# Fourth layer's sums turned by DMA instead of by TensorE in a four-layer graph network

## Chip, cores and metric

The kernel runs on one core of one Trainium2 chip. The metric is the device time of one execution in microseconds (us). Engines are called by the names of the profile: PE is TensorE's matmul, PEld its weight load, DVE is VectorE, ACT is ScalarE, POOL is GpSimd, SP is SyncE.

## What is computed

x is 3327 nodes by 256 features, adj a 3327 by 3327 matrix of zeros and ones. Four graph layers follow one another, each on `h = max(layernorm(x), 0)`, each added to x. The first is a graph attention, the second a normalized graph convolution, the third one with signs of weights and activations. The fourth, which the change touches, is

```
def _L3_gnn_ref(x, adj, t, weight):
    ts = t[0]
    support = x @ weight
    return (1.0 - ts) * support + ts * (adj @ support)
h = jnp.maximum(_layernorm(x, axis=-1), 0.0)
x = x + _L3_gnn_ref(h, adj, L3_gnn_t, L3_gnn_weight)
```

The kernel computes it as `z = (1 - ts) h + ts (adj @ h)`, then `x + z @ weight`.

## The kernel before

The 3327 rows are padded to 26 tiles of 128 nodes (`TILES`). In the fourth layer h is held in `x_layer[3]` as two f16 halves, a high part and the rest, so that the products are as exact as f32 asks for. For each tile t of 128 output rows TensorE makes 26 matmuls (`add3`, line 1495, one for each block j of 128 nodes), whose 512 columns are the 256 of the high half and the 256 of the low one. One f8 matrix block of the adjacency is the weight of each. They add up in one of four PSUM banks (`quarter`). `tile3` (line 1498) is the loop over j.

Then comes what the code calls the epilogue of tile t, on all engines while TensorE is already in tile t + 1:

- DVE `product` (lines 1866, 1869, 1871) makes z in `y_sb`, f32, from the two halves of the bank and the product `tb` that ACT made (line 1191), and raises `z_done[3]`.
- PE `layer_epilogue`, part 0, at j = 13 of the next tile: `turn` (line 1302) transposes z, two f32 matmuls with an identity of 128 by 128 each, into the PSUM bank `ep`, and raises `zt_psum[3]`.
- ACT `turned_copy` (line 1196) makes the high f16 half of the turned z in `zt16`, DVE `low3` (line 1910) the low one, and raises `zt_done[3]`.
- PE `layer_epilogue`, part 1, at j = 20 of the next tile: six f16 matmuls with the weight's halves `w3_16` (line 1376) into the bank `op`, then `p_done[3]`.
- DVE `update` (line 1903), in its order after `product` of the next tile, adds x and writes `xo`; SP stores it (line 823).

Which j a step stands at is written out by hand: `EPILOGUE_AT`, `LATE_AT` for tiles 2 and 3, `STEADY_AT` for all later ones. A value is (how many tiles back, which part, first or not).

DVE's order for tile t is `product(t)`, `update(t - 1)`, `low3(t)`, `check`. `check` (line 1856) goes over a half row block of the f32 adjacency in `gb`; the others of that kind have been done in the layers ahead. ACT's order is `turned_copy(t - 1)`, `product(t)`.

SP issues, when the matmuls of tile t are done (`mm_done[3]`): for odd t up to 17 one pair of adjacency tiles in f8, 832 KB, from a scratch tensor in HBM (`load_slot`, line 863); for each t up to 23 the next half row block for `check`, 832 KB (line 817); and the store of tile t - 2, 128 KB (line 823). All three run on SP's queue, q1 in the profile. ACT's queue (q10) carries five small loads at the very start and nothing else. ACT issues DMAs in its own instruction order.

Of the kernel before, what the change touches and what calls it, by code (L numbers as in the profile page):

```python
# [7 lines left out]
P = 128  # L8
# [458 lines left out]
def fast_program(nc, io, general, prefix="f_"):  # L467


    with ExitStack() as ctx:  # L470
# [3 lines left out]
        def sem(name):  # L474
            return ctx.enter_context(nc.semaphore(prefix + name))
# [40 lines left out]
        y_sb = sb("y_sb", [P, 2, 2 * F])  # L516
# [12 lines left out]
        xo = s_f32[:, 2304:2816].rearrange("p (r f) -> p r f", r=2)  # L529
        sign_w = s_flat[:, 5632:6144].rearrange("p (c f) -> p c f", c=FB)  # L530
        ident16 = s_flat[:, 6144:6272]
        binary = s_flat[:, 11264:11264 + 4 * F].rearrange("p (r f) -> p r f", r=4)
        w1_16 = s_flat[:, 8192:8192 + 4 * F].rearrange("p (h c f) -> p h c f", h=2, c=FB)
        binary_t = s_flat[:, 6784:7040]
# [162 lines left out]
        group_here = [sem(f"group_here{b}") for b in range(2)]  # L697
        yh_done = sem("yh_done")
        extra_here = [sem(f"extra_here{b}") for b in range(2)]
        slot_here = [sem(f"slot_here{b}") for b in range(4)]  # L700
        yl_done = sem("yl_done")
        w1_done = sem("w1_done")
# [66 lines left out]
        with nc.Block() as block:  # L769
# [197 lines left out]
            def _(a):  # L967
# [220 lines left out]
                def product(t, p, s):  # L1188
                    if not (isinstance(t, int) and t < 2):
                        a.wait_ge(z_done[3], t - 1)  # L1190
                    a.activation(tb[:, p * F:(p + 1) * F], x_layer[3][:, bass.ds(t, 1), F:2 * F].rearrange("p a f -> p (a f)"),
                                 ACT.Copy, scale=omt_scaled[:]).then_inc(tl_done[3], 1)

                def turned_copy(t):
                    a.wait_ge(zt_psum[3], t + 1)
                    a.activation(zt16[:, 0], ep[:, 0:F], ACT.Copy, scale=Z3).then_inc(zt_hi, 1)  # L1196

                def pair(k, s, first=False):
                    for p in range(2):
                        t = 2 * k + p  # L1200
                        if not (first and p == 0):
                            turned_copy(t - 1)
                        if first and p == 0:
                            product(0, 0, s)
                            product(1, 1, s)
                        if not first:
                            product(t, p, s)
                pair(0, 1, True)
                with a.Fori(0, PAIRS // 2) as k:
                    for i in range(2):  # L1210
                        pair(2 * k + 1 + i, i)
                turned_copy(TILES - 1)


            @block.tensor
            def _(pe):
# [139 lines left out]
                all_pairs(pe, pair)  # L1356

                def layer_epilogue(layer, t, p, part, first=False):
                    if part == 0:
                        turn(t, p, ep, zt_psum[layer], z_done[layer], FB)  # L1360
                    else:

                        if first:
                            pe.wait_ge(read_o[1], TILES)
                            pe.wait_ge(late_w, 64)
                        else:
                            pe.wait_ge(read_o[layer], t)
                        if layer == 1:
                            project(t, op, w_sb[layer], FB, zt_done[layer], p_done[layer])
                            return  # L1370
                        if first:
                            pe.wait_ge(w3_done, 2)
                        pe.wait_ge(zt_done[3], t + 1)
                        for c in range(FB):
                            for half, w_half in ((0, 0), (0, 1), (1, 0)):
                                mm = pe.matmul(op[:, 0:F], zt16[:, half, c * P:(c + 1) * P], w3_16[:, w_half, c, :],  # L1376
                                               start=(c + half + w_half == 0), stop=(c == FB - 1 and half == 1))
                        mm.then_inc(p_done[3], 1)

# [161 lines left out]
            def _(v):  # L1541
                def settle():

                    v.sem_inc(waited, 1)
# [314 lines left out]
                for layer in L:  # L1859
# [47 lines left out]
                    def low3(t):  # L1907

                        v.wait_ge(zt_hi, t + 1)
                        v.scalar_tensor_tensor(zt16[:, 1], ep[:, 0:F], Z3, zt16[:, 0], ALU.mult, ALU.subtract)\  # L1910
                         .then_inc(zt_done[3], 1)

                    def norm(t, p):

# [5 lines left out]
                    def pair(k, first, last=False, r=0):  # L1920
                        for p in range(2):
# [11 lines left out]
                            if layer == 3 and not (first and p == 1):  # L1933
                                product(t, p, r)
                                if first and p == 0:
                                    product(1, 1, r)
                                    low3(0)
                            if not (first and p == 0):

                                update(t - 1, 1 - p, k if p else k - 1, first)  # L1940
                            if layer == 3 and not (first and p == 0):
                                low3(t)
# [107 lines left out]
```

## Time and profile before

| | |
|---|---|
| median of 3 runs | 964.89 us (964.3 to 965.39) |
| profiled execution, whole | 965.67 us |
| its span, from first to last instruction | 964.0 us |
| PE busy | 933.9 us, 97% of the span |
| DVE busy | 743.3 us, 77% |
| ACT busy | 540.9 us, 56% |
| POOL busy | 94.1 us, 10% |
| mean granted TensorE clock | 0.988 of full |

Busy shares are means over four layers with different limits, so each stage is read from its own stretch of the trace. The fourth layer is the stretch from 779 us to the end; its steady tiles run from about 812 to 945 us.

### The profile page before, as it was taken

Reading aid. Unit: us, or ns where it says so; the run is one execution under the profiler, and the core shown is the slowest. Engines: PE = TensorE matmul, PEld = TensorE weight load, DVE = VectorE, ACT = ScalarE, POOL = GpSimd, SP = SyncE. Lnnn points to the kernel's source line nnn. Section 1 sums busy time; section 2 is a strip of 40 time slices with the busy share of each in tenths; the row PEclk is TensorE's granted clock in tenths of the full one; section 3 lists DMA queues with packets and bytes.
Section 4 is the critical chain, followed back from the end, with each engine's and each line's share of the span. In section 5 each row is a group of like instructions: output and inputs, shape, how many; then the busy total and the mean of one; then the engine's idle time right before and its main releaser. Section 6 shows DMA issues by size and latency. Waiting matters only on the chain.

```text
span 964.0 us, 18964 instructions
## 1 busy us (share of the span) xinstructions
PE 933.9 (97%) x7105; PEld 689.2 (71%) x7105; DVE 743.3 (77%) x1112; ACT 540.9 (56%) x934; POOL 94.1 (10%) x206
## 2 busy tenths in 40 slices
PE   9889999999999999999999999999999989999995
PEld 8457788888888888888888455555788845555553
DVE  7697899999999999999996776656447755655664
ACT  6476899999999999999985611111223331111010
POOL 4100001000010001000030000000024430000000
PEclk9899999999999999999999999999999999999998
DMA  4915276677576666658312425655247726666642
GB/s 178 96 45 77 23 100 76 66 89 96 48 96 83 81 66 86 86 51 109 46 39 100 173 94 203 211 183 203 114 181 281 276 79 213 215 227 205 201 153 65
DMA packets 39883, 120.80 MB, mean 125 GB/s; under 512 B 4604, under 2 KB 24597, under 8 KB 39701
## 3 DMA queue, kind: packets, MB, share of 16 engines
q1 hardware_dynamic: 27653, 97.94, 29.0%
q0 software_dynamic: 10944, 21.30, 25.5%
q10 hardware_dynamic: 1232, 0.85, 0.3%
q8 instruction: 32, 0.52, 0.2%
q14 instruction: 22, 0.18, 0.1%
HBM read 169.48 MB, written 14.50 MB: 191 GB/s over the span
## 4 chain that ended last, share of the span: by engine, by line
PE 84%; DVE 7%; ACT 3%; issue 2%; POOL 2%; DMA 0%; POOLq 0%; DVEq 0%; ACTq 0%
PE f_ya L1318 23%; PE f_yb L1318 23%; PE f_ya L1495 14%; PE f_ya L1433 12%; DVE f_gb L1856 2%; PE f_ya L1269 2%; PE f_yb L1404 2%; PE f_yb L1376 2%; PE f_yb L1269 1%; PE f_ya L1442 1%; POOL f_gv L960 1%; ACT f_ubuf L1184 1%; ACT f_x_mat L1186 1%; DVE f_stats L1600 1%; PE f_yb L1302 1%
## 5 line engine op out<-in xcount | busy, mean ns | idle before, releaser
L1318 PE MATMUL f_ya<-f_x_mat,f_s_mat 128*128 128x257 f16 x2028 | 334.6, 273 | 1.9 <-DVE f_x_mat L1664 1.9
L1318 PE MATMUL f_yb<-f_x_mat,f_s_mat 128*128 128x257 f16 x2028 | 333.2, 273 | 0.0
L1318 PEld LDWEIGHTS f_yb<-f_x_mat,f_s_mat 128*128 128x128 f16 x2028 | 198.2, 98 | 24.8
L1318 PEld LDWEIGHTS f_ya<-f_x_mat,f_s_mat 128*128 128x128 f16 x2028 | 194.5, 98 | 27.2 <-issue 2.8
L1030 ACT ACTIVATE f_gb<-f_e_tile,f_expc 128x256 f32<-128x256 f32 x338 | 144.5, 494 | 9.3 <-DVE f_s_mat L1694 9.3
L1856 DVE SCALAR_TENSOR_TENSOR f_gb<-f_gb 128x1664 f32<-128x1664 f32 x52 | 97.7, 1886 | 18.0 <-DMA f_gb<-adj_dram 18.0
L1689 DVE SCALAR_TENSOR_TENSOR f_s_mat<-f_wm,f_s_mat 128x1792 f16<-128x1792 f32 (+1 forms) x52 | 98.4, 1892 | 12.1 <-ACT f_s_mat L1041 8.5
L1683 DVE TENSOR_TENSOR f_wm<-f_gb,f_a 128x1792 f32<-128x1792 f32 (+1 forms) x52 | 98.1, 1887 | 3.2 <-issue 1.6
L1684 DVE SCALAR_TENSOR_TENSOR f_gb<-f_gb,f_a 128x1792 f32<-128x1792 f32 (+1 forms) x52 | 98.1, 1887 | 0.0
L1694 DVE SCALAR_TENSOR_TENSOR f_s_mat<-f_gb,f_s_mat 128x1792 f16<-128x1792 f32 (+1 forms) x52 | 98.0, 1886 | 0.0
L1041 ACT ACTIVATE f_s_mat<-f_wm 128x1792 f16<-128x1792 f32 (+1 forms) x52 | 82.5, 1587 | 22.0 <-DVE f_wm L1683 20.9
L1196 ACT ACTIVATE f_yt_sb<-f_yb 128x256 f16<-128x256 f32 x26 | 10.0, 384 | 145.2 <-PE f_yb L1302 145.2
L1495 PE MATMUL f_ya<-f_x_mat,f_wm 128*128 128x512 f16 x364 | 85.5, 385 | 3.6 <-DVE f_x_mat L1916 3.2
L1047 ACT ACTIVATE f_s_mat<-f_gb 128x1792 f16<-128x1792 f32 (+1 forms) x52 | 82.5, 1587 | 7.0 <-DVE f_gb L1684 6.9
L1433 PE MATMUL f_ya<-f_wm,f_x_mat 128*128 128x512 fp8e4 (+1 forms) x416 | 84.6, 352 | 0.0
L1056 ACT ACTIVATE f_rows<-f_rows 128x1664 fp8e4<-128x1664 fp8e4 x48 | 75.5, 1574 | 0.0
L1433 PE MATMUL f_ya<-f_a,f_x_mat 128*128 128x512 fp8e4 x312 | 73.1, 379 | 0.0
L1495 PE MATMUL f_ya<-f_x_mat,f_a 128*128 128x512 f16 x312 | 71.7, 379 | 0.0
L1495 PEld LDWEIGHTS f_ya<-f_x_mat,f_wm 128*128 128x128 fp8e4 x364 | 35.9, 99 | 42.6 <-DVE f_x_mat L1916 4.0
L1433 PEld LDWEIGHTS f_ya<-f_wm,f_x_mat 128*128 128x128 f16 x416 | 40.2, 98 | 32.6
L928 POOL DMA_DIRECT2D f_a<-adj_t_dram x52 | 28.4, 546 | 303.7 <-PE f_yb L1318 263.4
L1483 PE MATMUL f_ya<-f_s_mat,f_a 128*128 128x256 f16 x468 | 52.5, 272 | 3.5 <-DMA f_a<-f_a_dram 2.2
(185 smaller groups left out, 938.2 us busy)
## 6 DMA issues: line engine op xcount, KB each, us to landing
f_gb<-adj_dram SPq DMA_DIRECT2D x52, 832.0 KB, 5.0
f_a<-f_a_dram SPq DMA_DIRECT2D x23, 832.0 KB, 5.9
f_wm<-f_a_dram SPq DMA_DIRECT2D x16, 832.0 KB, 4.6
f_rows<-adj_dram POOLq DMA_DIRECT2D x24, 416.0 KB, 8.2
f_a<-adj_t_dram POOLq DMA_DIRECT2D x26, 224.0 KB, 4.9
f_a_dram<-f_a SPq DMA_DIRECT2D x26, 224.0 KB, 5.3
f_a<-adj_t_dram POOLq DMA_DIRECT2D x26, 192.0 KB, 6.9
f_a_dram<-f_a SPq DMA_DIRECT2D x26, 192.0 KB, 4.2
```

The costliest lines, as they stand in the source:

```text
L1030: made = a.activation(blocks(gb, c)[:, j - lo, :], e_tile[:, r, :], ACT.Copy, scale=expc[:, 0, j:j + 1])
L1041: a.activation(weights(c, 2), blocks(wm, c), ACT.Copy, scale=DOWN).then_inc(hm_done, 1)
L1047: a.activation(weights(c, 0), blocks(gb, c), ACT.Copy, scale=UP).then_inc(hp_done, 1)
L1056: a.activation(part_of, part_of, ACT.Copy, saturate=False, accum_out=row_parts[:, r, c:c + 1])\
L1318: return pe.matmul(bank[:, 0:F + 1], s_mat[:, j, side, i], x_mat[:, j, x_side, 0:F + 1], start=start, stop=stop)
L1433: mm = pe.matmul(turned_sum(g, f), x_layer[1][:, j, half * F + f * P:half * F + (f + 1) * P], wide[g % 2][:, 0:width(g) // HP, j, :], star ...
L1495: return pe.matmul(quarter[2 * s + p][:, 0:2 * F], slots3[slot][:, j, p * P:(p + 1) * P], x_layer[3][:, j, 0:2 * F], start=(j == 0), stop= ...
L1683: v.tensor_tensor(part(wm, c), part(gb, c), a8_part(r, c), ALU.min).then_inc(wm_done, 1)
L1684: v.scalar_tensor_tensor(part(gb, c), part(gb, c), 1.0, a8_part(r, c), ALU.max, ALU.mult).then_inc(wp_done, 1)
L1689: v.scalar_tensor_tensor(weights(c, 3), blocks(wm, c), DOWN, weights(c, 2), ALU.mult, ALU.subtract)\
L1694: v.scalar_tensor_tensor(weights(c, 1), blocks(gb, c), UP, weights(c, 0), ALU.mult, ALU.subtract)\
L1856: v.scalar_tensor_tensor(gb[:, half, 0:HW], gb[:, half, 0:HW], 0.0, gb[:, half, 0:HW], ALU.is_gt, ALU.not_equal, accum_out=bad[:, bass.ds( ...
```

## The change

In the fourth layer, for every tile but the last, z is no longer turned by TensorE. ACT makes the high f16 half of z straight from `y_sb` into a new buffer `z16`, DVE's `low3` makes the low half there too, and ACT issues, for each half and each of the two 128-column blocks, one transposing DMA (`transpose=True`) from `z16` to `z16_t`: two when the high half is there, and two after it has waited for DVE's low half. They are of 128 by 128 f16, 32 KB each, all four on one semaphore of the tile's parity, `z16_here[p]`. PE's six matmuls of line 1376 take their weights from `z16_t`, and stand at j = 24 of the next tile instead of j = 20, behind a wait for that semaphore. Nothing stands at j = 13. The first tiles are moved too: tile 0's six matmuls go to j = 22 of tile 2, tile 1's to j = 8 of tile 3, tile 2's to j = 24 of tile 3. ACT now makes `product(t + 1)` after it has issued the four transfers of tile t. Tile 25 goes the old way.

```diff
+                def high_part(t, p, n, reuse=True):
+
+                    a.wait_ge(z_done[3], t + 1)
+                    if reuse:
+                        a.wait_ge(z16_here[p], 64 * n)
+                        a.wait_ge(p_done[3], t - 1)
+                    a.activation(z16[:, p, 0, :], y_sb[:, p, 0:F], ACT.Copy, scale=Z3).then_inc(zt_hi, 1)
+                    a.wait_ge(zt_hi, t + 1)
+                    settle()
+                    for half in range(2):
+                        if half == 1:
+                            a.wait_ge(zt_done[3], t + 1)
+                            settle()
+                        for c in range(FB):
+                            a.dma_start(z16_t[:, p, half, c, :], z16[:, p, half, c * P:(c + 1) * P], transpose=True)\
+                             .then_inc(z16_here[p], 16)
...
-                pair(0, 1, True)
-                with a.Fori(0, PAIRS // 2) as k:
+                product(0, 0, 1)
+                product(1, 1, 1)
+                high_part(0, 0, 0, False)
+                high_part(1, 1, 0, False)
+                with a.Fori(0, PAIRS // 2 - 1) as k:
                     for i in range(2):
-                        pair(2 * k + 1 + i, i)
+                        for p in range(2):
+                            t = 4 * k + 2 + 2 * i + p
+                            product(t, p, i)
+                            high_part(t, p, 2 * k + 1 + i)
...
-                        pe.wait_ge(zt_done[3], t + 1)
+                        if at_end:
+                            pe.wait_ge(zt_done[3], t + 1)
+                        else:
+                            pe.wait_ge(z16_here[p], 32 * (t - p) + 64)
+                            settle()
                         for c in range(FB):
                             for half, w_half in ((0, 0), (0, 1), (1, 0)):
-                                mm = pe.matmul(op[:, 0:F], zt16[:, half, c * P:(c + 1) * P], w3_16[:, w_half, c, :],
+                                turned_z = zt16[:, half, c * P:(c + 1) * P] if at_end else z16_t[:, p, half, c, :]
+                                mm = pe.matmul(op[:, 0:F], turned_z, w3_16[:, w_half, c, :],
...
-                LATE_AT = ({13: (2, 0, False), 20: (2, 1, True)},
-                           {3: (2, 0, False), 8: (2, 1, False), 15: (1, 0, False), 22: (1, 1, False)})
-                STEADY_AT = {EPILOGUE_AT[3][i]: (1, i, False) for i in range(2)}
+                LATE_AT = ({22: (2, 1, True)}, {8: (2, 1, False), 24: (1, 1, False)})
+                STEADY_AT = {24: (1, 1, False)}
...
+                            v.scalar_tensor_tensor(z16[:, p, 1, :], y_sb[:, p, 0:F], Z3, z16[:, p, 0, :], ALU.mult, ALU.subtract)\
+                             .then_inc(zt_done[3], 1)
```

## Rows read from the trace of the kernel before

**Rows 1.** The page: busy time of each engine, and shares of the chain.
```profile
PE 933.9 (97%) x7105; PEld 689.2 (71%) x7105; DVE 743.3 (77%) x1112; ACT 540.9 (56%) x934; POOL 94.1 (10%) x206
PE 84%; DVE 7%; ACT 3%; issue 2%; POOL 2%; DMA 0%; POOLq 0%; DVEq 0%; ACTq 0%
```

**Rows 2.** The chain in order of time, from 720 us: start, us, what.
```profile
825.59 1.51 PE f_ya L1495 x7
827.10 0.66 PE f_yb L1376 x6
827.75 4.10 PE f_ya L1495 x19
832.07 1.51 PE f_ya L1495 x7
```

**Rows 3.** The timeline, 844.8 to 858.2 us: start, us, engine, line, what.
```profile
847.04 4.26 PE L1495 MATMUL f_ya<-f_x_mat,f_wm 128*128 128x512 f16 x19
...
848.53 0.33 SPq L863 DMA_DIRECT2D f_wm<-f_a_dram  x1
848.66 0.48 DVE L1869 SCALAR_TENSOR_TENSOR f_y_sb<-f_ya,f_t_scaled,f_s_mat 128x256 f32<-128x256 f32 x1 [0.52 <-PE f_ya L1495]
...
849.18 0.48 DVE L1871 SCALAR_TENSOR_TENSOR f_y_sb<-f_ya,f_t_scaled,f_y_sb 128x256 f32<-128x256 f32 x1
...
849.58 0.41 DVE L1903 SCALAR_TENSOR_TENSOR f_s_mat<-f_yb,f_xs 128x256 f32<-128x256 f32 x1
...
855.02 0.33 SPq L817 DMA_DIRECT2D f_gb<-adj_dram  x1
```

**Rows 4.** Groups by line, 700 to 964 us: count, busy us, mean ns, idle before.
```profile
L1302 PE MATMUL f_yb<-f_ident,f_y_sb 128*128 128x128 f32 x52 | 10.0, 274 | 1.2 <-DVE f_y_sb L1871 1.2
...
L1184 ACT ACTIVATE f_ubuf<-f_xs,f_down 128x256 f32<-128x256 f32 x26 | 13.2, 508 | 52.4 <-POOL f_cst L963 52.4
...
L1866 DVE SCALAR_TENSOR_TENSOR f_s_mat<-f_x_mat,f_omt_scaled,f_s_mat 128x256 f32<-128x256 f32 (+1 forms) x26 | 12.5, 481 | 0.1
```

**Rows 5.** DMA issues, 780 to 964 us: count, KB each, median us to landing.
```profile
f_wm<-f_a_dram SPq DMA_DIRECT2D x5, 832.0 KB, 4.5
f_a<-f_a_dram SPq DMA_DIRECT2D x4, 832.0 KB, 4.5
out_dram<-f_s_mat SPq DMA_DIRECT2D x25, 128.0 KB, 4.8
out_dram<-f_s_mat SPq DMA_DIRECT2D x1, 112.0 KB, 1.7
```

**Rows 6.** Stretches of 0.5 us; last columns: granted clock, DMA share, GB/s.
```profile
850.80:851.30 0.50, 0.50 (x5) 0.31 (x4) 0.00 (x0) 0.00 (x0) 0.00 (x0) 1.00 1.01 426
...
853.80:854.30 0.50, 0.50 (x4) 0.24 (x3) 0.50 (x3) 0.00 (x0) 0.00 (x0) 1.00 0.97 398
...
855.30:855.80 0.50, 0.50 (x4) 0.25 (x3) 0.47 (x2) 0.00 (x0) 0.00 (x0) 1.00 0.00 0
...
859.30:859.80 0.50, 0.50 (x7) 0.39 (x5) 0.50 (x1) 0.00 (x0) 0.00 (x0) 1.00 0.28 100
```

**Rows 7.** The start: page's queue row, landings (0 to 15 us), ACT's issues.
```profile
q10 hardware_dynamic: 1232, 0.85, 0.3%
...
f_s_mat<-w_att_t_dram ACTq DMA_DIRECT2D x1, 256.0 KB, 5.2
...
f_a_sb<-a_vec_dram ACTq DMA_DIRECT2D x1, 2.0 KB, 7.4
...
0.74 0.47 ACTq L971 DMA_DIRECT2D f_s_mat<-w_att_t_dram  x1
1.23 0.48 ACTq L972 DMA_DIRECT2D f_a_sb<-a_vec_dram  x1
...
2.23 0.81 ACTq L974 DMA_DIRECT2D f_wtrans_sb<-wtrans_dram  x1
```

**Rows 8.** Stretches of 2 us where TensorE waits; columns as in rows 6.
```profile
785.00:787.00 2.00, 0.23 (x1) 0.00 (x0) 0.73 (x3) 0.85 (x2) 1.60 (x6) 1.00 0.00 0
...
789.00:791.00 2.00, 2.00 (x6) 0.73 (x5) 0.77 (x2) 0.65 (x2) 0.00 (x0) 0.50 0.00 0
```

More of the change, by code:

```diff
@@ L531, in fast_program @@
         ident16 = s_flat[:, 6144:6272]
+        z16 = s_flat[:, 9216:9216 + 4 * F].rearrange("p (r h f) -> p r h f", r=2, h=2)
+        z16_t = s_flat[:, 10240:10240 + 4 * F].rearrange("p (r h c i) -> p r h c i", r=2, h=2, c=FB)
         binary = s_flat[:, 11264:11264 + 4 * F].rearrange("p (r f) -> p r f", r=4)
@@ L699, in fast_program @@
         extra_here = [sem(f"extra_here{b}") for b in range(2)]
+        z16_here = [sem(f"z16_here{b}") for b in range(2)]
         slot_here = [sem(f"slot_here{b}") for b in range(4)]
@@ L1194, in turned_copy @@
                 def turned_copy(t):
-                    a.wait_ge(zt_psum[3], t + 1)
+                    a.wait_ge(zt_psum[3], 1)
                     a.activation(zt16[:, 0], ep[:, 0:F], ACT.Copy, scale=Z3).then_inc(zt_hi, 1)
[L1198 to L1207, printed above, removed]
@@ L1212, in _ @@
+                for t in range(TILES - 4, TILES):
+                    product(t, t % 2, t // 2 % 2 ^ 1)
+                    if t < TILES - 1:
+                        high_part(t, t % 2, t // 2)
                 turned_copy(TILES - 1)
@@ L1358, in layer_epilogue @@
                 def layer_epilogue(layer, t, p, part, first=False):
+                    at_end = isinstance(t, int) and t == TILES - 1
                     if part == 0:
-                        turn(t, p, ep, zt_psum[layer], z_done[layer], FB)
+                        if at_end:
+                            turn(t, p, ep, zt_psum[layer], z_done[layer], FB)
                     else:
@@ L1372, in layer_epilogue @@
                             pe.wait_ge(w3_done, 2)
-                        pe.wait_ge(zt_done[3], t + 1)
+                        if at_end:
+                            pe.wait_ge(zt_done[3], t + 1)
+                        else:
+                            pe.wait_ge(z16_here[p], 32 * (t - p) + 64)
+                            settle()
                         for c in range(FB):
                             for half, w_half in ((0, 0), (0, 1), (1, 0)):
-                                mm = pe.matmul(op[:, 0:F], zt16[:, half, c * P:(c + 1) * P], w3_16[:, w_half, c, :],
+                                turned_z = zt16[:, half, c * P:(c + 1) * P] if at_end else z16_t[:, p, half, c, :]
+                                mm = pe.matmul(op[:, 0:F], turned_z, w3_16[:, w_half, c, :],
                                                start=(c + half + w_half == 0), stop=(c == FB - 1 and half == 1))
@@ L1905, in update, with low3 @@
                             v.nop().then_inc(read_o[3], 1)
-                    def low3(t):
+                    def low3(t, p):
                         v.wait_ge(zt_hi, t + 1)
-                        v.scalar_tensor_tensor(zt16[:, 1], ep[:, 0:F], Z3, zt16[:, 0], ALU.mult, ALU.subtract)\
-                         .then_inc(zt_done[3], 1)
+                        if isinstance(t, int) and t == TILES - 1:
+                            v.scalar_tensor_tensor(zt16[:, 1], ep[:, 0:F], Z3, zt16[:, 0], ALU.mult, ALU.subtract)\
+                             .then_inc(zt_done[3], 1)
+                        else:
+                            v.scalar_tensor_tensor(z16[:, p, 1, :], y_sb[:, p, 0:F], Z3, z16[:, p, 0, :], ALU.mult, ALU.subtract)\
+                             .then_inc(zt_done[3], 1)
                     def norm(t, p):
@@ L1936, in pair @@
                                     product(1, 1, r)
-                                    low3(0)
+                                    low3(0, 0)
                             if not (first and p == 0):
@@ L1941, in pair @@
                             if layer == 3 and not (first and p == 0):
-                                low3(t)
+                                low3(t, p)
                             if layer == 3 and not first and not (last and p == 1):
```

## The prediction, made blind

> **What bounds the kernel now.** I read the page first: PE is busy for 97% of the span and the chain that ended last runs over PE for 84% [rows 1]. Means of four layers say little about one, so next the chain in order of time, from 720 us on. In the fourth layer it repeats one pattern: 7 matmuls of line 1495, six of line 1376, 19 of line 1495, and again, with nothing but PE between [rows 2]. The reader is to see the small hole: 827.75 + 4.10 is 831.85, and the next piece starts at 832.07. Those 0.22 us are the two transposes of line 1302, which the chain leaves out as too short. One tile takes 832.07 - 825.59 = 6.48 us, and 26 x 0.216 (4.10 us / 19) + 0.66 + 0.216 is 6.49: there is no idle time in it. The layer goes at the pace of PE's instructions, so what is taken off PE is gained, and what PE waits for is lost in full.
>
> Next the timeline of one tile, for when z is there. In [rows 3] the 19 matmuls that start at 847.04 are the last 6 of one tile and the first 13 of the next, so the next tile begins at 847.04 + 6 x 0.216 = 848.34. I call that T, and count from it. DVE's first product starts at 848.66 and the second ends at 849.66: z is there at T + 1.32. SP issues its load at 848.53, T + 0.19.
>
> **What is removed.** 25 of the 26 pairs of transposes. A transpose shows 274 ns in the groups by line [rows 4], but they overlap their neighbours; what two of them take on PE is the hole of 0.216 us. 25 x 0.216 = 5.4 us come off PE. ACT's copy and DVE's low half are not removed, only moved: from after j = 13 to straight behind z. The six matmuls stay as they are, 0.66 us.
>
> **What is added, and when it is due.** The six matmuls now stand at j = 24, so the turned halves are due at T + 24 x 0.216 = T + 5.18. The path from z to there, T + 1.32 on:
> - ACT makes the high half from SBUF, f32 in. The copy from PSUM is no measure; the nearest row is line 1184, 0.51 us [rows 4]. With a few hundredths for the signal, T + 1.88.
> - Two issues. The trace has no transposing DMA, so I take plain ones on the same queue: ACT's first two start at 0.74 and 1.23 [rows 7], 0.49 us apart, and the longest takes 0.81. Lower bound 0.49 each, upper 0.81; I take 0.49, as most of ACT's issues are of that length.
> - DVE's low half meanwhile: `update` of the tile before ends at 849.99 [rows 3], T + 1.65, so DVE is free; from T + 1.88 it needs 0.48 (line 1866, SBUF sources [rows 4]), T + 2.4. ACT is then still issuing; the wait costs nothing.
> - The last of four issues starts at T + 1.90 + 3 x 0.49 = T + 3.37. A small transfer with nobody beside it, the last whole store, lands 1.7 us after its issue starts [rows 5]. T + 5.07.
>
> So with free DMA engines the halves come 0.1 us before they are due, and the stall is nothing. With an issue of 0.81 us it is T + 1.90 + 2.43 + 1.7 + 0.32 = T + 6.35, a stall of 1.2 us in each tile. Behind ACT's issues is queued `product(t + 1)`: 0.5 us, and DVE's line 1866 after it, ready by T + 4.9, where the next tile ends at T + 6.27. Covered by 1.4 us; with issues of 0.81 us the cover is 0.1. DVE's and SP's steps were not late before and have no new wait in the steady tiles.
>
> **What lies beside it.** The DMA engines are not free. SP's loads start at T + 0.19, just ahead. In the tile at 848.34 SP issued two loads of 832 KB and a store; the DMA share is 1.01 at 850.80 and still 0.97 at 853.80 to 854.30, and the engines are empty only at 855.3 [rows 6]. I call such a tile heavy; there are 9, since the load of the pair was issued 5 + 4 times [rows 5]. In the other 16, with one load (issued at 855.02 [rows 3]), the engines are as good as done at 859.3 [rows 6], T + 4.5 of that tile.
>
> How two queues share an engine can be read at the start. Queue q10 shows 1232 packets [rows 7], which is one for each row of its five loads (256 + 128 + 128 + 512 + 128 = 1152) and 16 for each completion (80): every row is a packet. `a_sb` is 2 KB in 128 rows, 8 rows and a completion for each of 16 engines. It is behind the 256 KB load on its queue, which landed at 0.74 + 5.2 = 5.9, and landed itself at 1.23 + 7.4 = 8.6 [rows 7]: 2.7 us for 9 packets of 16 bytes, 0.3 us each. SP was loading x then, rows of 6 KB and more, and such a row takes an engine 6144 B / (400 GB/s / 16) = 0.25 us at the rate that full engines show [rows 6]. So one large row of SP's went between each two small ones. I take the same for the transposes: 9 packets for each engine and block, 36 for a tile, each behind one large row as long as there are any. A small packet itself is 0.3% x 964 us x 16 / 1232 = 0.038 us [rows 7].
>
> Heavy tile: the first transfer's packets can start some 0.8 us after its issue at T + 1.9, at about 851.0. From there to 854.3 the engines are full at about 410 GB/s [rows 6]: 3.3 us x 410 GB/s is 1.35 MB, 85 KB for each engine, some 12 rows of 6.6 KB. 12 x (0.25 + 0.038) = 3.5 us, until 854.5; then the other 24 small ones and the store's 9, 33 x 0.038 = 1.25, and 0.3 for the last signal: 856.0. Due was 853.52. Stall 2.5 us. Light tile: SP is done at T + 4.5, the last block's packets come only at T + 4.2, and it lands at T + 5.1 to 5.3. Stall 0 to 0.1, taken as 0.
>
> The first tiles: DVE's `low3(1)` stands behind `update(0)`, and that now behind tile 0's matmuls at j = 22 of tile 2. So tile 1's low half is made about T + 6.3, its transfers land about 2.2 us into tile 3, where j = 8 is due at 1.7; and ACT's `product(2)` is queued behind those issues, which makes z of tile 2 some 1.7 us late and with it j = 24 of tile 3. Together about 2 us, once.
>
> **The sum.** -5.4 + 9 x 2.5 + 2 = +19.1 us. The profiled execution of 965.67 us would take 984.8, the median of 964.89 us 984.0. I forecast 984.
>
> By the Trainium skill, DMA: Bandwidth & Descriptors, section Queues, rings and completion order, an engine drains a whole packet of some 9 to 17 descriptors before it turns to another queue. By that rule a block would wait for one large row and not for nine, and the heavy stall would be about 0.5 us, the sum +1.1 us (the even case of rival 1 below); the trace does not agree for plain copies, where q10's packets count one for each row.
>
> **The rivals.**
> 1. No stall. The transfer is one or two packets for each engine, waits for one or two large rows at most and lands by T + 5.2 in heavy tiles too. Then -5.4 and 0 to 2 for the first tiles: 959.5 to 961.5 us. It is the other side, and it decides from T + 5.18. For it speaks that blocks with no neighbour come 0.1 us early; against it that nothing is left for a dearer issue or any wait. Chance 0.2. If the halves come 0.2 to 0.4 us late on average, the gain is used up and the time stays within 0.2% (963 to 966.8 us): 0.08.
> 2. The blocks go one after the other, each costing a whole small transfer. The row for one is 1.7 us [rows 5]: T + 1.9 + 4 x 1.7 = T + 8.7, a stall of 3.5 us in all 25 tiles, +88 - 5.4 + 2 = +84, 1049 us; with half of each 1.7 hidden behind the next issue it is near 1000. No row shows a transposing transfer, so nothing excludes it. Chance 0.22. The Trainium skill, VectorE: DVE Perf Modes, section The three transpose paths, gives 1309 ns for one 128 by 128 transpose by DMA; one after the other these are 5.2 us, and the estimate by that page would be near 1020 us. No run here shows it yet.
> 3. Slower still by TensorE's clock: where PE was busy for 0.23 of 2 us the granted clock was 0.50 soon after, 1.2 GHz [rows 8]. Stalls of 2.5 us could do that too. At half speed for 3.4 us a stall would cost 1.7 us more, +15 for nine, 999 us. This lies in the forecast's own range.
> 4. The transfers are no transposes by rows but element by element, 1024 packets of 0.038 us for each engine and block, 39 us each: milliseconds in all. Chance 0.02.
>
> **How the numbers follow.** The forecast's case, late in heavy tiles and perhaps a little in light ones, has 0.45 and a range of its own: from 970 (a heavy stall of 1.0 us) to 1003 (issues of 0.81 us: 16 light tiles x 1.2 = 19 us more). No stall 0.2, even 0.08, one after the other 0.22, other dearer ways 0.05. The range of 8 in 10 leaves out the upper half of rival 2, rival 4 and little of rival 1: 959.5 to 1030. Faster by over 0.2% (about what a measurement of this kernel can tell from no change) 0.2, within it 0.08, slower 0.72.
>
> **What would show it.** In the trace after: a steady light tile of 6.27 us on PE and no group of line 1302 but the last tile's; an idle time of PE ahead of line 1376 released by DMA, about 2.5 us in every second tile up to the ninth pair and near 0 in others; ACT's issues 0.49 us apart; the transfers' landing from 1.7 us in light tiles to 3 and more in heavy ones. If the issue lasts much longer than 0.5 us, or the transfers land later than 2 us with no load beside them, the term of 0.49 or 1.7 fails and rival 2 is near. If PE does not wait in heavy tiles, the one-to-one sharing of the engines fails.

## The result and the profile after

| | before | after |
|---|---|---|
| median of the runs shown together, us | 964.6 | 1053.88 |
| range of its runs, us | 961.8 to 965.39 | 1049.66 to 1059.53 |
| profiled execution, us | 965.67 | 1054.69 |
| its span, us | 964.0 | 1052.9 |
| mean granted clock of TensorE | 0.988 | 0.963 |

After over before is 1.0943, with an interval from 1.0898 to 1.0987: 89 us slower. The forecast was 984 us with a range up to 1030. The sign was right, the size was not: 19 us were foreseen.

First the page of after, its busy times and its chain by engine, for the whole program:

```profile
PE 956.9 (91%) x7055; PEld 689.1 (65%) x7055; DVE 745.4 (71%) x1112; ACT 544.3 (52%) x934; POOL 94.1 (9%) x206
...
PE 73%; DVE 7%; issue 6%; ACTq 4%; ACT 3%; DMA 3%; POOL 2%; DVEq 0%; POOLq 0%
```

PE had 84% of the chain [rows 1] and has 73%; ACT's queue, which had next to nothing, has 4%. So the fourth layer is no longer paced by PE alone. Next its groups by line, PE from 788 to 1053 us (busy us, mean ns of one | idle us ahead and what ended it):

```profile
L1522 PE MATMUL f_ya<-f_x_mat,f_wm 128*128 128x512 f16 x340 | 90.4, 429 | 2.5 <-DVE f_x_mat L1946 2.5
...
L1403 PE MATMUL f_yb<-f_s_mat 128*128 128x256 f16 x150 | 27.3, 334 | 66.1 <-issue 39.0 <-DMA f_s_mat<-f_s_mat 27.1
```

Line 1403 is line 1376 of before, and line 1522 is line 1495. The six matmuls on the turned halves now have 66.1 us of idle time ahead of them. The waits of the same stretch count them: 14 times put down to "issue" (no releaser found) and 11 times to the transfer into `f_s_mat`, 25 in all. Every tile whose sums are turned by DMA stalls, 2.6 us on average, not nine of them.

The windows tell the rest of the 89 us (busy us of PE, PEld, DVE, ACT and POOL, granted clock, DMA share, GB/s). Of after, from where the layer starts to its end:

```profile
790.00:1053.00 263.00, 187.24 (x808) 85.07 (x806) 99.13 (x178) 22.98 (x50) 0.00 (x0) 0.88 0.42 130
```

Of before, the same stretch of the program:

```profile
790.00:964.00 174.00, 164.22 (x858) 85.27 (x855) 97.07 (x178) 19.49 (x50) 0.00 (x0) 0.97 0.53 177
```

PE is idle for 263 - 187.24 = 75.8 us where it was 9.8: +66. It is busy for 23.0 us more with 50 instructions less. Since 5.4 us of work went, some 28 us are the slower clock, 0.88 instead of 0.97. 66 + 23 is 89.

Now one tile. The timeline of after, from 902 us, with SP's two loads (columns: start, us, engine, line, operation, count, [idle before and its releaser]):

```profile
902.59 5.34 PE L1522 MATMUL f_ya<-f_x_mat,f_a 128*128 128x512 f16 x24
902.78 0.33 SPq L866 DMA_DIRECT2D f_wm<-f_a_dram  x1
...
903.15 1.04 SPq L820 DMA_DIRECT2D f_gb<-adj_dram  x1
...
903.94 0.42 ACT L1203 ACTIVATE f_s_mat<-f_y_sb 128x256 f16<-128x256 f32 x1 [3.05 <-DVE f_y_sb L1897]
...
904.46 4.99 ACTq L1211 DMA_TRANSPOSE f_s_mat<-f_s_mat  x4
...
912.76 1.44 PE L1403 MATMUL f_yb<-f_s_mat 128*128 128x256 f16 x6 [4.83 <-issue]
914.00 7.53 PE L1522 MATMUL f_ya<-f_x_mat,f_a 128*128 128x512 f16 x26
```

T is 902.59. ACT starts the high half at 903.94, T + 1.35, behind a z that is just there, and has it at T + 1.77: as forecast. Then the four issues of line 1211 hold ACT's queue for 4.99 us, 1.25 us each, where the forecast had 0.49. The halves are there at about 912.6, T + 10.0 (in the chain PE starts 0.14 us after such a landing), and PE has waited since 907.93. The six matmuls then take 1.44 us instead of 0.66 [rows 2] and the next 26 take 7.53 instead of 5.6. The clock is seen in two windows just behind the stall, with the columns as above:

```profile
912.00:914.00 2.00, 1.24 (x7) 0.87 (x7) 0.00 (x0) 0.00 (x0) 0.00 (x0) 0.50 0.00 0
914.00:916.00 2.00, 2.00 (x6) 0.73 (x5) 0.76 (x2) 0.00 (x0) 0.00 (x0) 0.50 0.00 0
```

It is at 0.50, 1.2 GHz, after a stretch of 4.8 us in which PE did nothing. Not every stall ends so. Of the 25 groups of six, 12 took 1.16 us or more and 13 took 0.82 or less, and the length of the stall alone does not tell which:

```profile
932.92 0.82 PE L1403 MATMUL f_yb<-f_s_mat 128*128 128x256 f16 x6 [3.32 <-issue]
...
942.29 1.44 PE L1403 MATMUL f_yb<-f_s_mat 128*128 128x256 f16 x6 [2.94 <-DMA f_s_mat<-f_s_mat]
```

Around 933 the granted clock is 1.00, around 943 it is 0.50. From the one group to the next it is 9.37 us, the tile of after where the clock stays full.

The next tile has one load beside it. The chain of waits of after for it (start, us, what):

```profile
916.91 1.11 ACTq L1211
918.05 1.27 ACTq L1211
...
919.43 1.18 ACTq L1211
920.63 2.41 DMA f_s_mat<-f_s_mat
...
923.18 0.81 PE f_yb L1403 x6
```

The chain runs through ACT's queue: three issues, and then the fourth, which starts at 920.63 and whose transfer lands 2.41 us later. This tile began at about 914.9, so its halves are there at T + 8.1. Line 1211 over all of after:

```profile
L1211 ACTq DMA_TRANSPOSE f_s_mat<-f_s_mat x100: 1109/1263/1422, 797.1 to 1038.2; - x100
...
DMA to landing us min/median/max: 2.2/3.0/7.7
```

The shortest of a hundred issues takes 1.11 us. The longest plain one of before took 0.81 [rows 7].

### The profile page after: what moved, and what is told of

Its sections match the earlier page's. It is cut to its first block, busy times and chain, and to the rows that moved or that the text cites. A ratio compares the mean times of both kernels' runs of the same rounds, so it can differ in the third digit from the quotient of the medians.

```text
span 1052.9 us, 19038 instructions
## 1 busy us (share of the span) xinstructions
PE 956.9 (91%) x7055; PEld 689.1 (65%) x7055; DVE 745.4 (71%) x1112; ACT 544.3 (52%) x934; POOL 94.1 (9%) x206
## 4 chain that ended last, share of the span: by engine, by line
PE 73%; DVE 7%; issue 6%; ACTq 4%; ACT 3%; DMA 3%; POOL 2%; DVEq 0%; POOLq 0%
PE f_ya L1338 21%; PE f_yb L1338 21%; PE f_ya L1460 11%; PE f_ya L1522 9%; ACTq L1211 4%; PE f_yb L1403 3%; DMA f_s_mat<-f_s_mat 3%; DVE f_gb L1882 2%; PE f_ya L1289 2%; PE f_yb L1431 2%; PE f_yb L1289 1%; PE f_ya L1469 1%; POOL f_gv L963 1%; ACT f_x_mat L1189 1%; ACT f_ubuf L1187 1%
## 5 line engine op out<-in xcount | busy, mean ns | idle before, releaser
L1522 PE MATMUL f_ya<-f_x_mat,f_wm 128*128 128x512 f16 x364 | 95.9, 425 | 3.6 <-DVE f_x_mat L1946 3.2
L1403 PE MATMUL f_yb<-f_s_mat 128*128 128x256 f16 x150 | 27.3, 334 | 66.1 <-issue 39.0
L1194 ACT ACTIVATE f_s_mat<-f_x_mat,f_omt_scaled 128x256 f32 (+1 forms) x26 | 13.1, 506 | 128.9 <-issue 128.9
L1522 PE MATMUL f_ya<-f_x_mat,f_a 128*128 128x512 f16 x312 | 76.1, 403 | 0.0
L1522 PEld LDWEIGHTS f_ya<-f_x_mat,f_wm 128*128 128x128 fp8e4 x364 | 39.5, 109 | 55.6 <-issue 19.4
L1892 DVE SCALAR_TENSOR_TENSOR f_s_mat<-f_x_mat,f_omt_scaled,f_s_mat 128x256 f32<-128x256 f32 (+1 forms) x26 | 12.6, 484 | 87.0 <-ACT f_s_mat L1194 87.0
L1403 PEld LDWEIGHTS f_yb<-f_s_mat 128*128 128x128 f16 x150 | 15.3, 113 | 81.3 <-issue 77.9
```

Of the source, the lines that this page charges most:

```text
L1522: return pe.matmul(quarter[2 * s + p][:, 0:2 * F], slots3[slot][:, j, p * P:(p + 1) * P], x_layer[3][:, j, 0:2 * F], start=(j == 0), stop= ...
```

## The experiments

The theory that I formed from these rows, A: ACT's queue is held for 1.25 us by each transposing transfer, and four of them and a landing of 2.4 us make the path too long. The rival, B: the transfers queue behind the rows of SP's loads (the forecast's own mechanism, larger than forecast). A third, C: the fall of the clock makes the stalls dear.

### Only the form of the transfer: plain_copy

```
-  a.dma_start(z16_t[:, p, half, c, :], z16[:, p, half, c * P:(c + 1) * P], transpose=True)
+  a.dma_start(z16_t[:, p, half, c, :], z16[:, p, half, c * P:(c + 1) * P])
```

> The changed kernel with its four transfers of each tile made plain copies: the same 128 rows of 256 bytes from z16 to z16_t, on the same queue, with the same waits, but not transposed, so the fourth layer's last product takes unturned weights and its numbers are not the reference's. Theory A (the transposing form is dear to issue: 1.25 us each on ACT where I took 0.49, and lands in 2.4 where I took 1.7): the issues fall to 0.45-0.5 us, the copies land by T + 5.1 in a light tile and about T + 7.3 in a heavy one; 9 x 2.1 - 5.4 + 2, about 980 us (970 to 985). Theory B (what costs is the sharing of the DMA engines with SP's loads, row by row): the rows are the same, so the time stays near 1050 us, above 1035 in any case.

Measured: 1016.17 us, 1.0525 (1.0502 to 1.0547). Its issues and landings, line 1211:

```profile
L1211 ACTq DMA_DIRECT2D f_s_mat<-f_s_mat x100: 472/613/704, 797.1 to 1004.1; - x100
...
DMA to landing us min/median/max: 1.7/3.1/6.1
```

Half of the issue time is gone and 38 of the 89 us, not the 70 and more that A said; B's 1035 us and more is missed as well. Its chain, in a tile with two loads:

```profile
889.84 5.61 PE f_ya L1522 x26
895.45 3.70 issue
899.15 1.44 PE f_yb L1403 x6
900.59 7.77 PE f_ya L1522 x26
```

T is 890.1 here, and even copies, whose last issue is over at T + 4.4, land at T + 8.9. The tile behind it does not stall, but its 26 matmuls ran for 7.77 us at the low clock: the halves had 2 us more time. So B has a share too, and a tile without a stall in such a kernel is not proof that its transfers were in time.

### Only the load beside: small_checks

The load of the check, 832 KB in each tile, takes 16 columns of them; the check then looks at old data for the rest.

```
-  load_check(q + 14, p, t + 28)
+  load_check(q + 14, p, t + 28, cols=16)
```

> The changed kernel with the half row blocks that SP loads for DVE's check in the fourth layer cut from 1664 to 16 columns: DVE checks what already lies in the buffer, so part of the test of the adjacency is left out; all else is computed. No tile has two large loads now, 9 have one, 16 have none. Theory A: a light tile's four issues and its landing are the same, T + 8.0; only heavy tiles gain, some 1 to 2 us each: 1035 to 1045 us. Theory B: most of the stall goes, 965 to 985 us.

Measured: 1046.53 us, 1.0845 (1.0826 to 1.0863). Only 7 us come back, a little less than A said, though the median landing is 2.4 us now. B alone is out.

### Half of the transfers: high_only

> The changed kernel with only the high half's two transfers; they are issued when the low half is made too, and the six matmuls take the high half's weights where they took the low one's, so the low half of z is left out of the result. Theory A: two issues fewer, 2.5 us off the path of each tile: issues at T + 2.35 and 3.6, landing at T + 6.0 in light tiles, where 5.18 is due, and about T + 8 in heavy ones; stalls of 0.8 and 2.8 us, too short for the clock to fall: 16 x 0.8 + 9 x 2.8 - 3.4, about 1000 us (990 to 1010). Theory B: half the rows, half the stall, and no dependence on the light tiles' issues: near 1010 us too, but with stalls in heavy tiles alone.

Measured: 1013.63 us, 1.051 (1.049 to 1.0529). Two transfers for a tile instead of four bring 40 us back. The time does not tell A from B, which gave 990 to 1010 and near 1010, but the stalls side with A: they are 2.6 to 3.5 us in the nine tiles with two loads, and 0.6 to 1.3 in each of the last six, where B had none. What A had at nothing is the clock, for which it took these stalls as too short: behind the one of 2.7 us at 826 it was 0.58 in the mean of 2 us, and the 26 matmuls that then run at the low clock hide the short stall of the tile after them.

### Both of these, and later: plain_small, one_per_half

plain_small has the copies of plain_copy and the small loads of small_checks.

> Both suspected causes taken away: the four transfers are plain copies (the last product gets unturned weights), and SP's loads for the check are 16 columns wide (part of the test of the adjacency is left out). If the dear issue and SP's loads are the whole of it, the copies land by T + 5.1 to 5.4 and only the 9 tiles with the pair's load stall, by 1 us or less: 962 to 975 us. If either alone were the cause, this would be no better than that kernel alone (1016 or 1047 us); if there is a third cause, over 985 us.

Measured: 983.86 us, 1.0198 (1.0178 to 1.0218), a miss by 9 us. PE waits 24 times for 19.1 us in all: 0.2 to 0.5 us in most tiles, and 0.7 to 2.8 in those where the load of a pair, 832 KB, stands beside the copies. Of the three longest, one of 1.7 us is tile 2's; it stands in plain_alone (below) too, where no load is beside it, and so belongs to the order of the first tiles.

one_per_half keeps the transposition but makes one transfer of 256 columns out of two of 128:

```
-  for c in range(FB):
-      a.dma_start(z16_t[:, p, half, c, :], z16[:, p, half, c * P:(c + 1) * P], transpose=True)\
-       .then_inc(z16_here[p], 16)
+  a.dma_start(z16_t[:, p, half, :, :], z16[:, p, half, :], transpose=True).then_inc(z16_here[p], 16)
```

> The changed kernel with one transposing transfer of 128 rows by 256 columns for each half, in place of two of 128 columns; the same bytes turned, the complete computation. Theory A1 (the 1.25 us is a price for each instruction): two issues of about 1.3 us, the last starting at T + 3.2, landing at T + 5.8 to 6.2 in light tiles: 1000 to 1015 us, as with the high half alone (1013.6). Theory A2 (it is a price for each 128 by 128 block, worked off while ACT stands): two issues of 2.2 to 2.5 us, the same landing as the changed kernel: 1045 to 1058 us.

Measured: 1013.37 us, 1.05 (1.0485 to 1.0516), as A1 said. Its issues, now line 1210:

```profile
L1210 ACTq DMA_TRANSPOSE f_s_mat<-f_s_mat x50: 1184/1200/1428, 796.2 to 997.8; - x50
```

Twice the columns, the same 1.2 us. The price is one for the instruction and not for the block, and the same work is 40 us cheaper in half as many. What is left, in its chain, with the load of a pair beside it in the second tile:

```profile
861.52 7.30 PE f_ya L1520 x26
868.82 0.65 PE f_yb L1401 x6
...
872.93 4.99 DMA f_s_mat<-f_s_mat
```

The transfer issued at 872.93 lands 4.99 us later, where the shortest landing of this form is 2.3 us. I then took the tile at 861.52 for one that needs no help; its 7.30 us show the low clock again, and the next run showed what that hid.

### One transfer for each half with less beside it: one_small, one_slot_deferred

> One transposing transfer for each half, and SP's loads for the check 16 columns wide (part of the test of the adjacency is left out). In the kernel with one transfer for each half alone (1013.4 us) a light tile did not stall and a heavy one stalled 3.0 us with the clock at half behind it. If the heavy stall is the row-by-row sharing with SP's second load, nine tiles are now like light ones and the others have free engines: no stall in steady tiles, 961 to 967 us. If a heavy tile stalls for another reason than the bytes beside it, 990 us or more.

Measured: 982.95 us, 1.0196 (1.0178 to 1.0215), between its two ranges and 16 us above the first: the heavy tiles still stall, 0.7 to 2.9 us. Its waits on PE (us in total, times, longest):

```profile
PE f_yb L1401 <- issue: 15.1, 13, 2.8
PE f_yb L1401 <- DMA f_s_mat<-f_s_mat: 5.7, 11, 0.8
```

At the full clock even a tile with nothing large beside it is 0.5 us late: ready at T + 5.85. So two transposing transfers do not fit ahead of j = 24 either.

one_slot_deferred leaves the check loads as they were and lets SP issue the load of a pair only when the odd tile's halves are there.

> One transposing transfer for each half; SP issues the pair's load of a heavy tile only after that tile's transposed halves have landed, behind its other load and the store; nothing is left out. The halves then meet one load only in their own tile, but the rest of the pair's load lies at the start of the next tile, ahead of its check load. Sharing theory: the heavy stall of 3.0 us goes and the next tile stalls by 0 to 1.5 us: 962 to 985 us. If the place of the load does not matter: 1005 to 1018 us.

Measured: 1009.33 us, 1.0463 (1.0438 to 1.0488). That is in the range for a load whose place does not matter. The stall moved to the next tile's transfer, which the chain has at 879.87 with 4.83 us to land, where the heavy tile's own, at 872.38, took 2.84. As many bytes come in a pair of tiles, and wherever they are put, some transfer lies beside them.

### The cost of the clock: fillers

24 matmuls on old data, into a PSUM bank that nobody reads then, ahead of the wait of the six:

```
+  for _ in range(24):
+      pe.matmul(yb[0, 1][:, 0:F], x_layer[3][:, 0, 0:P], x_layer[3][:, 0, 0:F], start=True, stop=True)
```

> The changed kernel with 24 matmuls of 128 by 256 f16 into an unused bank ahead of each wait for the transposed halves, about 2.6 us that lie in the stall; the complete computation. Theory C (some 28 us of the 89 are TensorE running at half clock behind the longer stalls): the clock stays at 1.00, tiles stall about 2.9 and 5.0 us to the same landings: 1020 to 1032 us. Rival (the clock's fall is a side effect that costs nothing, as the stall shrinks by what the slower matmuls take): 1050 to 1056 us.

Measured: 1046.16 us, 1.0836 (1.082 to 1.0851), between the two ranges and in neither. The mean granted clock rose from 0.963 to 0.984. Of the 28 us by which PE's matmuls are longer at the low clock, the fillers bring back 8. That is a lower bound: PE still waits behind the fillers in 17 tiles, and in the other 8 the fillers, 2.6 us and more, hold the six matmuls back themselves. From above, an estimate: between the landing and the next tile lie the six matmuls and two more, 1.44 + 0.87 us at the low clock against 0.82 + 0.45 in the chain of after, so 12 slow tiles put 12 us on the path. This agrees with plain_copy's unstalled tile: matmuls at the low clock run while the next transfers are under way, and what they take longer is taken off the next stall.

### Neither load beside: turned_alone, plain_alone

What the pairs above leave open is how much the form costs alone. Both kernels have the check loads cut to 16 columns and the pair's loads to 64; turned_alone transposes as after does, plain_alone copies.

```
-  load_slot(q + 4)
+  load_slot(q + 4, 64)
```

> The changed kernel with SP's loads of the fourth layer cut to a few columns, both the check's (16) and the pairs' (64 of 6656), so that the transposing transfers have the DMA engines to themselves; most of the layer multiplies what lies in the slots from before, and part of the adjacency's test is left out. Issue theory: four issues of 1.25 us and a landing of 2.4, landed at T + 8.05 in every tile, a stall of 2.9: 25 x 2.9 - 5.4 + 2 = +69, 1030 to 1040 us. Sharing theory: under 1000 us.

Measured: 1046.21 us, 1.0872 (1.0832 to 1.0913), 6 us above the range of the issue theory and far from the other.

> The same with the four transfers as plain copies (the last product gets unturned weights as well). Issue theory: issues of 0.5 to 0.6 us, landed at T + 5.5 to 5.7, a stall of 0.3 to 0.5: +5 to +10, 970 to 975 us; nothing but issue and landing of the copies is left, and the difference to the kernel with the transposing form, 60 to 65 us, is the whole price of that form on this path. If the copies too were much later with free engines, over 985 us, something that neither theory has is on the path.

Measured: 973.1 us, 1.0097 (1.0068 to 1.0126), as expected; the difference, 73 us, is more than the 60 to 65 that were. Line 1211 of turned_alone:

```profile
L1211 ACTq DMA_TRANSPOSE f_s_mat<-f_s_mat x100: 1109/1231/1267, 796.8 to 1029.0; - x100
...
DMA to landing us min/median/max: 2.2/2.4/2.5
```

and of plain_alone:

```profile
L1211 ACTq DMA_DIRECT2D f_s_mat<-f_s_mat x100: 472/582/634, 794.0 to 955.8; - x100
...
DMA to landing us min/median/max: 1.7/1.8/1.9
```

These two pairs of rows are the cleanest prices in this case. Three issues longer by 0.65 us each and a landing longer by 0.6 are 2.55 us a tile, 64 us (an estimate from these medians); the other 9 us fit the clock, a mean of 0.965 here and 0.994 in plain_alone. And a tile of turned_alone, its chain of waits, where the clock is low behind both stalls:

```profile
876.07 1.35 PE f_yb L1403 x6
...
879.46 0.42 ACT f_s_mat L1203
...
879.99 1.11 ACTq L1211
881.12 1.27 ACTq L1211
...
882.51 1.17 ACTq L1211
883.71 2.39 DMA f_s_mat<-f_s_mat
...
886.24 1.28 PE f_yb L1403 x6
```

From one group of six to the next it is 886.24 - 876.07 = 10.2 us, where before a tile took 6.48 [rows 2]; and the chain goes round through DVE, ACT, ACT's queue and the transfer with hardly a matmul in it. The layer runs at the pace of this path. Ten of its 25 tiles take 10.1 to 10.4 us, each with the low clock behind its stall, and most of the others 9.0 to 9.4.

The kernels that differ in form, width and load alone, in a table (medians, us):

| transfers of a tile | loads as in after | check loads small | both loads small |
|---|---|---|---|
| 4 transposing | 1053.88 | 1046.53 | 1046.21 |
| 2 transposing, twice as wide | 1013.37 | 982.95 | |
| 4 plain copies | 1016.17 | 983.86 | 973.1 |

The causes do not add. With slow issues the loads cost 8 us (first row), with quick ones 43 (third row); the form costs 73 us with nothing beside it and 38 beside the loads. A late issue and busy DMA engines are two ends for the same wait, and PE sees the later. In the heavy tile of after the fourth transposing transfer is issued at T + 5.7, when by the windows some two thirds of SP's bytes have gone; it lands 4.4 us later, 2.0 more than alone, and in light tiles 2.4. The last copy of plain_copy's heavy tile is issued at T + 3.8, in the middle of them, and lands 5.1 us later, 3.3 more than alone.

### Consumer later: later_and_ahead, later_tail, later_tail_one

The other way is to leave the issues as they are and to need the result later. later_and_ahead puts the six matmuls behind j = 22 of the tile after next, makes `update` of two tiles before, and lets ACT and DVE make the product two tiles ahead, so that the product is not queued behind four issues:

```
-  STEADY_AT = {24: (1, 1, False)}
+  STEADY_AT = {22: (2, 1, False)}
...
-  update(t - 1, 1 - p, k if p else k - 1, first)
+  update(t - 2, p, k - 1, isinstance(k, int) and k == 1)
```

> The changed kernel with tile t's six matmuls at j = 22 of tile t + 2 and its update behind product(t + 2), all four transfers as they are, and ACT's product(t + 2) issued right behind high_part(t), two tiles ahead of its need; the complete computation. Theory A in its full form (latency on PE's path, not throughput): due is T + 6.27 + 4.75 = T + 11.0, landed by T + 8.0 to 10.2, so no stall; ACT is busy for 5.0 + 0.51 + 0.42 + 0.2 = 6.1 us of each tile's 6.27. -5.4 us for the transposes, +1 to 3 at the end where tile 24's products come late: 961 to 964 us. Theory D (ACT's own time sets the pace: if waits and issue under load add over 0.2 us, each tile takes ACT's 6.4 to 6.8): 965 to 978 us. Theory B: the transfers slow SP's loads or are slowed without bound: over 1000 us.

Measured: 975.83 us, 1.0122 (1.0101 to 1.0143), in the range of D. 78 of the 89 us are gone with every issue still there. PE waits 12 times, 12.6 us in all, 2.8 and 3.4 us the longest. ACT's work for a tile is 0.51 + 0.42 + 5.0 us of issues and gaps, 6.1 to 6.3 us: as long as PE's tile, so that a hitch on ACT's queue has little room before it reaches PE. And at the end two tiles' halves have nothing left to hide behind.

later_tail mends the end: tiles 24 and 25 are turned on TensorE as before, and the six stand behind j = 25.

> Tile t's six matmuls at j = 25 of tile t + 2, ACT's products two tiles ahead, and tiles 24 and 25 turned by TensorE; the complete computation. Against the version at j = 22 (975.8 us) the transfers have 0.65 us more, which covers the 0.4 to 0.5 us that every second tile lacked, and the end loses its wait for tile 24, 6 us. Theory A: 963 to 967 us, so no faster than the kernel before, since ACT's 6.1 us a tile leaves no room. Theory D (ACT's loop with the landings paces the layer, wherever the matmuls stand): only the end is gained, 968 to 971 us.

Measured: 975.96 us, 1.0101 (1.0081 to 1.0121), with runs from 969.76 to 981.77; both expectations missed. Its chain:

```profile
811.92 5.61 PE f_ya L1524 x26
817.53 4.15 issue
821.69 1.44 PE f_yb L1405 x6
...
830.44 0.66 PE f_yb L1405 x6
831.10 5.61 PE f_ya L1524 x26
```

Most tiles take the 6.27 us of the forecast (0.66 + 5.61), but in four places the layer stalls for 2.3 to 4.2 us. One issue of line 1211 took 2.5 us in this kernel, and with ACT full there is hardly any slack to take that up. What holds ACT in those places is open; with half the issues, in the next kernel, three of the four are gone.

later_tail_one is the same with one transfer for each half, which halves ACT's issues:

> Tile t's six matmuls at j = 25 of tile t + 2, ACT's products two tiles ahead, tiles 24 and 25 turned by TensorE, and one transposing transfer for each half; the complete computation. ACT's tile falls from 6.1 to 3.6 us, and the halves start 1.2 us earlier and land by T + 8.5 in heavy tiles, due at T + 11.7. The stalls of 2 to 4 us that the version with four transfers had in three places (975.9 us) had their cause in ACT's full tile plus an instruction fetch beside two loads, so they go: 965.0 - 5 + 1 at the first tiles, 959.5 to 963 us, faster than the kernel before. If those stalls come from the engines' sharing alone, 965 to 972 us.

Measured: 960.73 us, 0.9972 (0.996 to 0.9984), 12 runs from 958.95 to 962.99 against 964.2 for before, as expected. The chain of waits, tile after tile:

```profile
895.32 5.61 PE f_ya L1522 x26
900.93 0.66 PE f_yb L1403 x6
901.58 5.61 PE f_ya L1522 x26
```

and line 1210, its transfers:

```profile
L1210 ACTq DMA_TRANSPOSE f_s_mat<-f_s_mat x48: 1184/1206/1395, 794.2 to 936.0; - x48
...
DMA to landing us min/median/max: 2.3/4.3/7.6
```

Issues of 1.2 us, landings of up to 7.6 us beside SP's loads, and a tile of 901.58 - 895.32 = 6.26 us: PE waits for the halves once, 2.3 us, in the first tiles. The idea of the change is right by 0.3%; what cost 9% was where its result was wanted, and in how many pieces it was made. (Here 24 pairs of transposes are saved, not 25, and tile 24 is turned by TensorE too.)

## Why the prediction was right and wrong

**Failed: the issue.** The step is "Two issues": "Lower bound 0.49 each, upper 0.81; I take 0.49". Measured: 1.11 to 1.42, median 1.26. The upper bound was that of a plain transfer, and a row of another form is no bound for this one. The prediction said of rival 2 that no row shows a transposing transfer and nothing excludes it, but let the bounds stand in its own sum; and its range up to 1030 left out just the half of that rival in which the time fell.

**Failed: the landing.** 1.7 us was taken from a store; a transposing transfer with nothing beside it needs 2.4. Put both in the prediction's own path: T + 1.90 + 3 x 1.25 + 2.4 = T + 8.05, and the chain of after shows T + 8.1. Due was T + 5.18. That is 2.9 us in each of 25 tiles, 72 us, where the forecast had nothing in 16 of them. With 0.14 us from the landing to PE, the six matmuls and two more, the tile of after at the full clock is 9.37 us (from 932.92 to 942.29); 25 x (9.37 - 6.27) - 5.4 is 72 us. turned_alone is 81 us above before, and its tiles of 10.2 us show what is missing: the eight matmuls at the low clock behind some of the stalls.

**Undersized: the loads.** The heavy stall of 2.5 us stood on a path with quick issues; plain_copy has that path, and its heavy tile stalls 3.7 us (2.9 to 4.6 in all of them) and lands at T + 8.9 instead of T + 7.7. In after this term is nearly covered by the issues: 7.7 us in all (turned_alone to after), where the forecast's nine heavy tiles were to carry the whole loss. That the transfers wait for SP's loads is borne out by the landings: 2.4 us with free engines, up to 7.7 beside the loads. That they wait row by row, one small packet after one large row, is not shown by any run. (The sum took the engines as full at 410 GB/s; the windows of before from 850.8 to 854.3 us have a mean of 390, which changes nothing.) For the number of packets the queue's row of after, from 780 us (packets, MB, share of 16 engines), is this:

```profile
q10 hardware_dynamic: 16000, 3.29, 6.3%
```

16000 over 100 transfers are 160 for each. The same reading gives 144 for a plain copy of the block and 288 for the transfer twice as wide. That fits one packet for each row of a block, with 16 besides for each plain copy and for each transposed block 32; thousands for each block, as the element-wise rival has it, are out. By the Trainium skill, DMA: Bandwidth & Descriptors, section Queues, rings and completion order, an engine drains a whole packet of some 9 to 17 descriptors from one queue before it turns to another. The prediction took from this that a block waits for one large row, 0.5 us in all. But the rule is as good for SP's queue: if each of SP's rows is a descriptor, a turn of that queue is 9 to 17 rows of the prediction's 0.25 us, 2.3 to 4.3 us by an estimate from that page's figure. The last copy in plain_copy's heavy tile lands 3.3 us later than with free engines, so the trace does not speak against the rule, and no run here tells the two orders apart.

**Rival 2 had the number, 1049 us, and half the mechanism.** It let the blocks go one after another with 1.7 us each. What is serial is the issuing, 1.25 us each on ACT's queue; the transfers overlap, since the next issue starts long before the last one has landed. That the price is one for each instruction one_per_half shows, where twice the columns take the same 1.20 us. Two of the rival's sums do not follow from the prediction's own terms: with half of each 1.7 us hidden the last block lands at T + 6.15, which is 986 us and not near 1000, and four blocks of 1309 ns end at T + 7.1, a stall of 2.0 us in 25 tiles, which is 1010 us and not near 1020. The Trainium skill, VectorE: DVE Perf Modes, section The three transpose paths, gives 1309 ns for a 128 by 128 transpose by DMA. The issue rows agree with that figure (1.11 to 1.42); the time to landing does not, 2.2 us at the least. The estimate from it was nearer than the forecast, and what it leaves out is the landing behind the fourth issue.

**Rival 3, the clock**, is there: it is low behind 12 of the 25 stalls, 28 us on PE's busy time. But most of that is hidden by the next transfers: fillers bring back 8 us, and by the rows the path is longer by some 12. The rival's 1.7 us for a stall would be 20 us for those 12.

**Right:** the path up to the issues (high half at T + 1.77, forecast T + 1.88), the 5.4 us that PE saves (a tile of 6.26 us in later_tail_one), and that DVE's and SP's own steps are covered. ACT's product was late by ACT's issues, but within PE's stall. "Light 0" was wrong even for copies: in plain_alone the stall is 0.3 to 0.5 us in each tile, so the forecast's 0.1 us of slack was none. The 2 us of the first tiles can be read in plain_alone: its first three stalls are 0.7, 1.0 and 1.7 us, 3.4 in all, where three later ones make about 1.1. In after they lie within the 66 us of stalls.

## What to carry to other kernels

Before a transfer replaces work of an engine, cost its issue on the queue of the engine that issues it, count the instructions and not the bytes, and give an unseen form a bound from above that is not the row of a known form. Make a transposing transfer as wide as it goes, and put its consumer by its landing beside the busiest load, here two tiles later, rather than at the last place of the same tile. Where two causes end at one wait, the price of each depends on the other, so vary them together.

## What the runs showed of the hardware

- A transposing transfer from SBUF to SBUF holds ACT's queue for 1.11 to 1.27 us, median 1.23, with nothing beside it, where a plain one of the same block takes 0.47 to 0.63, median 0.58. 256 columns in one cost as much as 128.
- It lands 2.2 to 2.5 us after its issue starts, a plain one 1.7 to 1.9, when the engines are free.
- It counts 160 packets in its queue's row where a plain copy of the block counts 144, and 288 when it is twice as wide.
- TensorE's clock stood at 0.50 behind a stall of 4.8 us, and the 26 matmuls there took 7.53 us; it stood at 0.50 behind one of 2.9 us and at 1.00 behind one of 3.3. Keeping PE busy in the stalls raised the mean from 0.963 to 0.984, for a gain of 8 us.
- Beside SP's two loads of 832 KB a plain copy issued in the middle of them landed 3.3 us later than alone, and a transposing transfer issued when two thirds of their bytes had gone 2.0 us later.
